# The last block's attention results in the score banks, its filler matmuls removed, and the tail's instructions in another order

## The reference, cut to what matters

```python
x = x + 0.5 * ffn(_layernorm(x))
x = x + linear_attention(_layernorm(x))      # 16 heads of 32
x = x + 0.5 * ffn(_layernorm(x))
...
# linear_attention, per head, token after token:
S = S + phi_k[:, None] * v[None, :];  z = z + phi_k
out = (phi_q @ S) / (phi_q . z + EPS)        # phi(u) = elu(u) + 1
# then out @ Wo.T + bo
```

## Time and profile before

| What | Value |
|---|---|
| median of 3 runs | 933.25 us (933.16 to 933.83) |
| the profiled execution | 931.69 us |
| its span, first to last instruction | 929.8 us |
| mean granted TensorE clock | 0.996 |
| TensorE busy | 900.6 us, 97% |
| VectorE busy | 832.3 us, 90% |
| ScalarE busy | 756.8 us, 81% |
| GpSimd busy | 705.3 us, 76% |

### The profile page before, as it was taken

The page is one execution under the profiler, slowest core; times in us unless marked ns, Lnnn a source line. Parts: engine busy times, 40 slices in busy tenths (PEclk is TensorE's granted clock), DMA queues, the critical chain, the costliest instruction groups (busy, mean ns, idle before and its releaser), DMA issues.

```text
span 929.8 us, 30016 instructions
## 1 busy us (share of the span) xinstructions
PE 900.6 (97%) x10278; PEld 527.0 (57%) x10278; DVE 832.3 (90%) x1539; ACT 756.8 (81%) x1323; POOL 705.3 (76%) x869
## 2 busy tenths in 40 slices
PE   4999999999999999999999999999999999999995
PEld 3455555655555665555565655556555556555562
DVE  6989898999999999999999999999999999988885
ACT  6988888888888888888888888888888888888752
POOL 1469777779777778877778977777887777897661
PEclk9999999999999999999999999999999999999999
DMA  8576698876677767668767667776766876766873
GB/s 292 94 152 133 141 179 160 150 138 151 147 162 159 162 138 150 151 143 180 158 146 143 148 147 160 159 165 137 154 147 144 176 158 150 142 129 125 155 121 69
DMA packets 421421, 139.82 MB, mean 150 GB/s; under 512 B 402560, under 2 KB 402560, under 8 KB 421376
## 3 DMA queue, kind: packets, MB, share of 16 engines
q1 hardware_dynamic: 404496, 106.73, 61.6%
q10 hardware_dynamic: 16880, 32.51, 10.6%
HBM read 21.76 MB, written 16.78 MB: 41 GB/s over the span
## 4 chain that ended last, share of the span: by engine, by line
PE 85%; DVE 5%; DMA 4%; ACT 2%; issue 2%; POOL 1%; SPq 0%; ACTq 0%; POOLq 0%; DVEq 0%
PE PJ L1564 48%; PE PJ L1675 17%; PE AV L1643 8%; PE SC L1616 6%; PE AV L1661 5%; PE AV L1640 2%; DMA AT<-ATTN 2%; DMA A<-in_L_attn_Wk_dram 1%; DMA KS<-KN 1%; ACT Y L622 1%; DVE TP L1273 1%; DVE AM L1151 1%; DVE wT L1065 0%; DVE Y L1282 0%; ACT QN L722 0%
## 5 line engine op out<-in xcount | busy, mean ns | idle before, releaser
L1564 PE MATMUL PJ<-wT,XT 128*128 128x512 f16 x2304 | 524.8, 380 | 1.4 <-DMA XT<-XH 0.6
L1564 PEld LDWEIGHTS PJ<-wT,XT 128*128 128x128 f16 x2304 | 216.9, 98 | 245.4 <-issue 3.9
L490 POOL TENSOR_TENSOR A<-AM,A 128x512 f16<-128x512 f32 x252 | 288.2, 1164 | 32.1 <-ACT A L757 32.1
L1675 PE MATMUL PJ<-wT,AT 128*128 128x512 f16 x768 | 176.1, 379 | 2.7 <-DMA AT<-ATTN 2.6
L480 POOL TENSOR_SCALAR_AFFINE_SELECT AM<-AM 128x512 f32<-128x512 f32 x124 | 79.6, 642 | 113.1 <-ACT AM L744 113.1
L757 ACT ACTIVATE A<-AM 128x512 f16<-128x512 f32 x256 | 154.0, 631 | 12.3 <-POOL AM L480 8.9
L1675 PEld LDWEIGHTS PJ<-wT,AT 128*128 128x128 f16 x768 | 71.1, 97 | 80.1 <-DMA AT<-ATTN 4.1
L1643 PE MATMUL AV<-VN,A 128*128 128x33 f16 x3072 | 116.2, 178 | 0.0
L1640 PE MATMUL AV<-SS,QS 128*128 128x33 f16 x1024 | 111.6, 178 | 1.2 <-DVE TP L1216 1.2
L1643 PEld LDWEIGHTS AV<-VN,A 128*128 128x128 f16 x3072 | 108.8, 96 | 3.5
L1151 DVE TENSOR_TENSOR AM<-SC,causal 128x512 f32<-128x512 f32 x132 | 89.7, 682 | 18.2 <-PE SC L1616 18.2
(11 more groups left out here) (106 smaller groups left out, 1574.9 us busy)
## 6 DMA issues: line engine op xcount, KB each, us to landing
out_dram<-Y ACTq DMA_DIRECT2D x31, 512.0 KB, 3.2
X<-in_L_attn_x_dram ACTq DMA_DIRECT2D x30, 512.0 KB, 3.5
X<-in_L_attn_x_dram SPq DMA_DIRECT2D x2, 512.0 KB, 8.0
A<-in_L_attn_Wk_dram SPq DMA_DIRECT2D x1, 1024.0 KB, 8.0
A<-in_L_attn_Wq_dram SPq DMA_DIRECT2D x1, 1024.0 KB, 10.2
QS<-in_L_attn_Wv_dram SPq DMA_DIRECT2D x1, 1024.0 KB, 12.4
QS<-in_L_attn_Wo_dram SPq DMA_DIRECT2D x1, 1024.0 KB, 15.9
XT<-XH SPq DMA_TRANSPOSE x64, 3.5
```

Of the source, the lines that this page charges most:

```text
L490: g.tensor_tensor(A[:, b, LO, hg], AM[:, k % 4], A[:, b, HI, hg], ALU.subtract).then_inc(a_lo.sem, 1)
L1564: ins = t_.matmul(PJ[b], XT[:, w, c, b * C:(b + 1) * C], wT[m_][:, m, c, :], start=(c, w, m) == todo[0], stop=(c, w, m) == todo[-1])
L1675: ins = t_.matmul(PJ[b], AT[:, b, w, c * C:(c + 1) * C], wT[3][:, m, c, :], start=(c, w, m) == todo[0], stop=(c, w, m) == todo[-1])
```

## The change

It alters the written-out `closing` of four engines (SyncE's calls stay), and four places of the operations:

- in step 31 the quotients go to SC[b] instead of TP[b], and wait for the last masked score instead of the block before's `back_y`; the two splits read them there;
- `keep_busy` and its 26 matmuls in step 31 are gone;
- the final norm of sequence 1 of block 31 is done in two halves of 256 columns, in TP[1] and SC[0], with a store each;
- `back_scale` of the last two blocks waits for the `back_y` before it, as nothing else protects TP[b] now.

The diff, cut to its core:

```diff
-            sp.wait_ge(y_stored.sem, y_stored.at(steps - 1, 1))
+            sp.wait_ge(y_stored.sem, y_stored.at(steps - 1, 2))
...
# scalar
+                    def back_scale_part(h):
+                        half = slice(h * E // 2, (h + 1) * E // 2)
+                        act.wait_ge(*rstd2_done.upto(back, 1))
+                        act.wait_ge(*attn_lo.upto(back, 1))
+                        act.wait_ge(*y_done.upto(st.chunk(-2), 1))
+                        a.activation((TP[1], SC[0])[h][:, half], gain[:, half], ACT.Identity, bias=1.0, scale=rstd2[:, 1:2]).then_inc(g2_done.sem, 1)
+
+                    def store_part(h):
+                        half = slice(h * E // 2, (h + 1) * E // 2)
+                        act.wait_ge(*y_done.upto(back, 1 + h))
+                        a.dma_start(out[1, bass.ds(back * C, C), half], Y[:, 1, half]).then_inc(y_stored.sem, 16)
...
                             act.wait_ge(*attn_lo.upto(back, b))
+                            if not ATTEND:
+                                act.wait_ge(*y_done.upto(st.chunk(-2), b))
...
-        a.activation(ATTN[:, b, HI], TP[b][:], ACT.Copy, scale=ATTN_UP)
+        a.activation(ATTN[:, b, HI], (TP if PROJECT else SC)[b][:], ACT.Copy, scale=ATTN_UP)
...
                 third.k_half(1)
-                third.store_y()
                 third.q_half(0)
...
                 third.attn_half(1)
-                second.split_a(0, 1)
-                second.split_a(0, 2)
-                third.v_half(1)
                 second.split_a(0, 3)
+                third.store_y()
                 second.split_a(1, 0)
+                third.v_half(1)
+                third.s_half(0)
...
                 second.attn_half(0)
                 second.sums(1)
                 second.attn_half(1)
+                second.back_scale(0)
+                second.back_scale(1)
                 second.store_y()
                 last.back_scale(0)
-                last.back_scale(1)
+                last.back_scale_part(0)
+                last.back_scale_part(1)
                 last.store_tile(0)
-                last.store_tile(1)
+                last.store_part(0)
+                last.store_part(1)
...
# vector, quotient(b)
-                        if FINISH:
+                        if FINISH and PROJECT:
                             dve.wait_ge(*y_done.upto(back, b))
+                        elif PROJECT:
+                            dve.wait_ge(*x1_done.upto(f, b))
                         else:
-                            dve.wait_ge(*x1_done.upto(f, b))
+                            dve.wait_ge(*sc_masked.upto(s, BATCH * GROUPS - 1))
...
# vector, step 30: fourth.x_low(1) moves behind a mask
-                fourth.x_low(1)
-                fourth.add_out(0)
                 third.mask(0, 2)
+                fourth.x_low(1)
+                fourth.add_out(0)
...
# tensor
-                    def keep_busy(n):
-                        pe.wait_ge(*x2_done.upto(back, 0))
-                        for i in range(n):
-                            t_.matmul(PJ[0], wT[0][:, HI, 0, 0:P], wT[0][:, HI, 0, :], start=True, stop=True)
...
                 second.scores(0, 1)
+                third.attend(1, 0)
                 second.scores(0, 2)
-                third.attend(1, 0)
+                second.scores(0, 3)
                 third.attend(1, 1)
-                second.scores(0, 3)
                 third.project_v(1)
                 second.scores(1, 0)
-                second.scores(1, 1)
                 third.update(1, 0)
                 third.update(1, 1)
+                second.scores(1, 1)
+                second.scores(1, 2)
                 third.project_out(0)
+                second.scores(1, 3)
                 third.project_out(1)
-                second.scores(1, 2)
-                second.scores(1, 3)
                 second.attend(0, 0)
                 second.attend(0, 1)
-                second.keep_busy(14)
                 second.attend(1, 0)
                 second.attend(1, 1)
-                second.keep_busy(12)
                 second.project_out(0)
                 second.project_out(1)
```

More of the change, by code:

```diff
@@ L1487, in closing @@
                 third.attn_low(1)
+                second.mask(1, 0)
                 second.split_a(0, 1)
+                second.mask(1, 1)
                 third.low_v(1)
+                second.mask(1, 2)
                 third.add_s(1)
-                second.mask(1, 0)
-                second.mask(1, 1)
                 second.split_a(0, 3)
@@ L1521, in closing @@
                 last.back_y(0)
-                last.back_gain(1)
-                last.back_y(1)
+                last.back_gain_part(0)
+                last.back_gain_part(1)
+                last.back_y_part(0)
+                last.back_y_part(1)
             closing()
@@ L1766, in closing @@
                 third.scores(0, 0)
-                third.scores(0, 1)
                 fourth.update(1, 0)
                 fourth.update(1, 1)
+                third.scores(0, 1)
                 fourth.project_out(0)
@@ L1776, in closing @@
                 third.project_q(0)
+                third.attend(0, 0)
                 third.scores(1, 0)
@@ L1780, in closing @@
                 third.scores(1, 2)
-                third.attend(0, 0)
                 third.attend(0, 1)
```

123 lines of the change are left out of this document (66 added, 57 removed).

## The result

| | before | changed |
|---|---|---|
| median, same chip, 6 runs each | 933.58 us (933.16 to 934.92) | 930.36 us (929.37 to 931.00) |
| ratio | | 0.9963 [0.9945, 0.9981] |
| the profiled execution, its span | 931.69, 929.8 us | 930.95, 929.1 us |
| mean granted TensorE clock | 0.996 | 0.994 |

The kernel is 3.2 us faster at the medians, 1.3 us short of the 929.1 that was forecast and inside the range. In two later comparisons the unaltered changed kernel came out at 0.9974 [0.9955, 0.9993] and 0.9977 [0.9960, 0.9994], some 2.1 to 2.4 us. Between the fastest and the slowest execution of one kernel in one batch lie 1.6 to 9.4 us, so medians don't settle parts of a microsecond here; landmarks in the traces do, one trace for each kernel.

The account below looks back on a forecast made before the run. TensorE, busy 97% of the span, was taken as the bound, with the last step's waits running through VectorE. Terms 1.1 + 2.8 + 0 + 0 + 0.2 + 0 gave 4.1 us faster, 929.1 us from 933.25; range 927.0 to 932.7.

Parts of the forecast that it names:

- A: Up to the end of step 31's first `attend`: hidden mask wait and held clock gain 1.1 us, range 0 to 2.0.
- B: First to second `attend` of step 31: quotient no longer behind the final norm, 2.8 us gained, range 1.5 to 2.9.
- rival 3: Before the second `attend`, VectorE's in-order work delays the quotient: 930.4 us; shares chance 0.56 with the forecast.
- C: Second `attend` to first output projection of step 31: no change, 0 within 0.6 us.
- D: Step 31's two output projections: shorter transpose wait offset by clock fall, 0; +1.35 us if the clock holds.
- E: Tail behind the last projection: final norm and store in halves gain 0.2 us, range -0.3 to 0.6.
- F: Everything else moved in steps 29 and 30: 0, down to -0.7 us, with `x_low(1)` ending later.
- Rival 1: The clock holds through the last step, worth +1.35 us at the output projections: 927.8 us; chance 0.18.
- Rival 2: Both last projections at half clock and step 30's early hole stays: 933.1 us, same as before; chance 0.19.
- Rival 4: Waiting for Q of sequence 1 drops the clock, which stays low without filler: 938.2 us, slower; chance 0.07.

Follow-up runs that it names:

- e4: The kernel before with its 26 filler matmuls taken out of the last step, nothing else changed; 933.97 us, 1.0007 of before.
- e2: The changed kernel with steps 29 and 30 in the order of the kernel before, keeping the new last step; 931.96 us, 0.9977 of before.
- e6: The changed kernel with sequence 1's `x_low` again ahead of the mask that waits for scores; 931.23 us, 0.9964 of before.
- e8: The changed kernel itself, unaltered, run again; 931.74 us, 0.9974 of before.
- e5: The kernel before with only the last step's quotients moved to the score banks and their waits changed, order and filler kept; 934.91 us, 1.0016 of before.
- e3: The changed kernel with filler put back, 6 matmuls after the last step's first `attend` and 14 after the second; 931.81 us, 0.9974 of before.
- e9: The changed kernel with `x_low` ahead of the mask and filler of 6 and 8 matmuls in the last step's two gaps; 929.81 us, 0.9966 of before.
- e10: The changed kernel with `x_low` ahead of the mask and filler of 6 and 14 matmuls in the last step's two gaps; 930.81 us, 0.9975 of before.
- e1: The changed kernel with only block 29's store moved earlier, amid the transposes of block 31's K and Q; 932.49 us, 0.9989 of before.
- e11: The changed kernel with `x_low` ahead of the mask and 6 filler matmuls in the last step's first gap only; 930.55 us, 0.9976 of before.

## Why the prediction was right or wrong, point by point

**A, the way to the first `attend` of step 31: forecast +1.1 us, measured -0.5, -1.0 and -1.1 in the three traces of the changed kernel. This is the step that failed.** Its parts:

- The 0.56 us of the mask are hidden, and V's projection is back at 2.75, as said. Neither counts, since TensorE only arrives earlier at the wait for Q of sequence 1. e4 shows the same without any of the change.
- "The queue is emptier: I take a landing at 895.9": this is the term that was mis-sized. It landed at 899.3 in the execution that starts 1.6 us later, 24.8 after P30 instead of the 23.0 of the forecast (24.3 before). Two errors are in it. The transpose took 6.2 us and not 5.2: its length isn't set by the store (e2 and e4 have it in front and take 6.6, e6 and e8 don't and take 6.3 and 6.2), but goes with the fetch in it. And I took its issue as fixed. It came 18.6 us after P30, 17.8 before, since the two issues in front of it on SyncE took 3.0 each, where before one took 1.8.
- The wait for Q of sequence 0 was "0.48, since they end with the landing". It became 1.32, as that transpose took 5.6 us where before it took 4.7.
- TensorE's own arrival was put at 895.4; the 1.6 us taken from 897.43 give 895.8. It changes nothing, as the landing was taken as later than either.
- The 0.4 us for the store ahead of the transpose of sequence 1's result (a landing 4.4 us after the issue) did not come: it landed in 3.8, at 902.3, and the projection that needs it began at 903.69 without a wait.
- The end of the range, "0, the late landing or the clock falls anyway", had no case in which the landing comes later than before. That was too narrow: nothing in the profile excluded it.

**B, first to second `attend`: +2.8, measured 2.80** in every trace with the new order (6.06 to 3.26). The margin of 0.05 was as near as forecast: denominators ready at 908.37, mask over and reciprocal started at 908.40. So rival 3's delay didn't occur. e5 confirms its core: with the bank alone the program order keeps VectorE busy elsewhere, and 0.2 is left.

**C: 0, measured +0.1** (4.93 to 4.84).

**D, the two projections: forecast 0, measured -0.4, +0.3 and -0.1.** The size is right and the two opposite terms are both there: the transpose at 3.1 instead of 4.4, and a low clock. But the reason given for the first, no store in front, is refuted by e3 and e4. The clock fell at about 911.7, for 6.8 us instead of the 3.4 taken; TensorE was idle in 2.6 of them, and before that it had been idle for 1.47 with 1.6 of `attend` behind it. The two projections took 7.41, 2.1 more than at full clock, where 1.7 were forecast (6.67, so 1.3, in e8). The page "TensorE: Matmul & The Clock Gate" of the Trainium skill, Part 1, has throttled as the default and activity as what releases it; the slices agree, 0.74 at 911.5 in the idle stretch and 0.93 at 918.5 under dense matmuls. What going by that rule alone misses is that filler pays for itself only if nothing else rides on it; here the price came back through the second transpose.

**E, the tail in halves: +0.2, measured 0.3** (7.57 to 7.27). Six operations of 0.46 to 0.49 us. The half stores landed in 1.8 to 1.9 us against 2.1 for 256 KB, so halving saved 0.2 to 0.3; the slope of the earlier trace rows had promised 0.5, a landing in 1.6.

**F: 0, "down to -0.7".** The wait for `x_low`'s transpose came in two of the three traces of the changed kernel, 0.64 and 0.65 us. It is part of the -1.0 and -1.1 above; e6 removes it. The low end of this term was right, and it came only where a fetch fell into that transpose.

**The sum.** With A at -0.5, B 2.8, C 0.1, D -0.4 and E 0.3 the first trace gives 2.3, the other two 2.5 and 1.9. The first comparison's 3.2 (by its interval 1.8 to 5.1) includes these, as do the later 2.4 and 2.1. The forecast's 4.1 was too much by what A was off, 1.6 or more. That the first median came within 1.3 us of the forecast is in part luck: 3.2 is the largest gain of the three comparisons and lies above what any trace gives, and in D two terms of more than 1 us cancelled as they were priced, one of them for a wrong reason.

**The rivals.** Rival 1, a warm clock worth +1.35: its premise was brought about in e3, e9 and e10, and O to R gained at most 0.6 over the first trace of the changed kernel and nothing over its second (6.71). The clock's gain and the transpose's are not independent, which the forecast took them to be. Rival 2 came nearest on A, which it let be 0, and had the last step too cold. Rival 4 had a real mechanism, the clock lost at the wait for Q: V's projection of step 30 runs partly or wholly at the low level in the third trace of the changed kernel (3.68 us) and in e1, e3, e9, e10 and e11 (3.45 to 4.18). But each time it came back under the dense work that follows, and the time lay in the wait for the transpose anyway.

What stays open: whether moving the instruction fetch alone takes 1.3 us from either transpose, why the transpose of Q of sequence 0 takes 5.4 to 5.8 us in the new order and 4.6 to 5.1 in the old one, and why SyncE's transposes take 1.7 us to issue in one place and 3.0 in another.

## What to carry to other kernels

Before you credit a stall that you remove, or a clock that you restore, look up when the next wait ends and what sets it: here 1.6 us of TensorE time in step 30 were real and worth nothing, since a transpose landed when it landed. If a wait is tied to a chain of DMAs, forecast the issue of the last one too, and keep the case that it moves later in the range. Where a transfer lands late, look whether the instruction queue has a packet beside it. And a bank freed is worth only the program order that it allows: write the order so that the operation which others wait for comes first.

## What the runs showed of the hardware that was not expected

- A packet of the instruction queue within a transpose goes with 1.3 us more until it lands: 3.0 to 3.1 us without in eight traces, 4.3 to 4.7 with it in six. Ahead of 890 us and outside the loop the medians are 3.3 without (127 transposes) and 4.3 with it (97), and in the loop, 201 to 800 us, where no such packet is, 3.1. Fourteen to twenty-six matmuls that only keep TensorE active can bring one more such packet.
- A store of 512 KB just in front of a group of transposes costs them nothing (15.2 to 15.4 us for four, against 15.3 to 15.8 without); in the middle of the group the trace has 1.9 us or more of cost (e1).
- Twenty-six filler matmuls less, with TensorE idle for 4.27 us before the second `attend`, change the time by 0.07% with an interval that includes 0 (e4).
- The clock of the same program differs between executions: V's projection of step 30 took 2.75 us, at full clock, in two traces of the changed kernel and 3.68, partly at the low one, in the third.
